# A three-layer graph attention kernel: the first layer's input split into two fp32r parts, score columns on VectorE

## What is computed

```python
def _L0_gnn_ref(h, adj, W, a):                      # layer A
    Wh = jnp.matmul(h, W)
    e_i = jnp.einsum('bnf,f->bn', Wh, a1)
    e_j = jnp.einsum('bnf,f->bn', Wh, a2)
    e = jax.nn.leaky_relu(e_i[:, :, None] + e_j[:, None, :], negative_slope=ALPHA)
    e = jnp.where(adj == 0, MASK_VAL, e)
    attention = jax.nn.softmax(e, axis=2)
    return jax.nn.elu(jnp.matmul(attention, Wh))
...
def gat_layer(x, mask, W, a_src, a_dst, bias, concat):   # layers B and C
    xl = (x @ W).reshape(B, N, H, F)
    asrc = jnp.einsum('bnhf,hf->bnh', xl, a_src)
    adst = jnp.einsum('bnhf,hf->bnh', xl, a_dst)
    e = jax.nn.leaky_relu(asrc[:, :, None, :] + adst[:, None, :, :], NEG_SLOPE)
    e = jnp.where(mask[..., None], e, NEG_INF)
    attn = jax.nn.softmax(e, axis=1)
    out = jnp.einsum('bsdh,bshf->bdhf', attn, xl)
...
x = _layernorm(x + _L0_gnn_ref(x, adj, L0_gnn_W, L0_gnn_a), axis=-1)
x = _layernorm(x + _L1_gnn_ref(adj, x, ...), axis=-1)
```

## Time and profile before

| | |
|---|---|
| median of 3 runs | 668.99 us |
| profiled execution, device time | 667.11 us |
| its span (first to last instruction) | 665.2 us |
| PE, PEld, DVE busy | 637.9, 574.9, 588.7 us (96%, 86%, 88%) |
| ACT, POOL busy | 482.0, 448.6 us (72%, 67%) |
| DMA | 45.68 MB at 69 GB/s on average |
| mean granted clock of PE | 0.988 of full speed |

### The profile page before, as it was taken

The page is one execution under the profiler, slowest core; times in us unless marked ns, Lnnn a source line. Parts: engine busy times, 40 slices in busy tenths (PEclk is TensorE's granted clock), DMA queues, the critical chain, the costliest instruction groups (busy, mean ns, idle before and its releaser), DMA issues. The chain is left out here.

```text
span 665.2 us, 17485 instructions
## 1 busy us (share of the span) xinstructions
PE 637.9 (96%) x4156; PEld 574.9 (86%) x4156; DVE 588.7 (88%) x2315; ACT 482.0 (72%) x1220; POOL 448.6 (67%) x811
## 2 busy tenths in 40 slices
PE   6979999999999999999999999999999999999993
PEld 5758899998999999999999989999999999988871
DVE  1488999999999999999999999999999999899953
ACT  1457887787778777777787777778877777687661
POOL 0247577777777777677777777777777777666762
PEclk9999999999999999999999999999999999999996
DMA  8311112222212222221122222211222222210001
GB/s 269 96 48 36 46 49 80 81 65 81 67 37 75 81 81 80 65 81 62 40 77 81 81 67 78 81 48 50 80 81 80 65 80 73 89 33 0 18 17 47
DMA packets 46693, 45.68 MB, mean 69 GB/s; under 512 B 2817, under 2 KB 46337, under 8 KB 46594
## 3 DMA queue, kind: packets, MB, share of 16 engines
q1 hardware_dynamic: 45648, 43.79, 20.8%
q10 hardware_dynamic: 946, 0.80, 0.4%
HBM read 36.19 MB, written 8.39 MB: 67 GB/s over the span
## 5 line engine op out<-in xcount | busy, mean ns | idle before, releaser
L378 POOL TENSOR_SCALAR probB<-probB,rdenB 128x256 f32<-128x256 f32 x256 | 124.7, 499 | 79.9 <-DVE rdenB L958 79.6
L558 ACT ACTIVATE probB<-probB,shiftB 128x256 f32<-128x256 f32 x256 | 127.1, 499 | 16.8 <-DVE shiftB L927 13.0
L1524 PE MATMUL PS<-probTB,VB 128*128 128x256 f32 x512 | 128.2, 382 | 0.9 <-ACT probTB L577 0.8
L941 DVE SCALAR_TENSOR_TENSOR probB<-PS,VB,gatedB 128x256 f32<-128x256 f32 x256 | 111.5, 478 | 1.8 <-issue 0.4
L389 POOL TENSOR_TENSOR inlC<-hidT,inhC 128x512 fp32r<-128x512 f32 x64 | 82.0, 1281 | 43.7 <-ACT inhC L622 43.6
L899 DVE CUSTOM_DVE_ANT_0 gatedB<-PS,gate_bc 128x256 f32<-128x256 f32 x256 | 93.8, 420 | 7.3 <-PE PS L1494 5.5
L1524 PEld LDWEIGHTS PS<-probTB,VB 128*128 128x128 f32 x512 | 89.3, 190 | 11.0 <-ACT probTB L577 2.1
L1480 PE MATMUL PS<-WhB,inhB 128*128 128x260 f32 x256 | 81.8, 319 | 1.4 <-DVE inlB L972 1.2
L577 ACT ACTIVATE probTB<-PS 128x512 f32<-128x512 f32 x128 | 72.9, 591 | 9.9 <-PE PS L1505 9.6
L360 POOL TENSOR_TENSOR y<-y,xres 128x512 f32<-128x512 f32 x32 | 41.1, 1286 | 52.4 <-DVE y L963 52.4
L1480 PE MATMUL PS<-WhC,inhC 128*128 128x258 f32 x256 | 75.4, 294 | 0.5 <-issue 0.4
(11 more groups left out here) (108 smaller groups left out, 1626.1 us busy)
## 6 DMA issues: line engine op xcount, KB each, us to landing
adj_in<-in_adj_dram SPq DMA_DIRECT2D x32, 256.0 KB, 4.3
xTin<-in_x_t_dram SPq DMA_DIRECT2D x32, 256.0 KB, 4.1
adjT_in<-in_adj_t_dram SPq DMA_DIRECT2D x32, 256.0 KB, 3.1
xres<-in_x_dram SPq DMA_DIRECT2D x32, 256.0 KB, 2.8
out_dram<-res SPq DMA_DIRECT2D x32, 256.0 KB, 2.1
WTC<-in_L_gnn_W_t_dram SPq DMA_DIRECT2D x1, 512.0 KB, 7.4
WTB<-in_L_gnn_W_t_dram ACTq DMA_DIRECT2D x1, 512.0 KB, 8.0
WB<-in_L_gnn_W_dram SPq DMA_DIRECT2D x2, 256.0 KB, 8.3
```

The lines of the kernel that those rows point to most:

```text
L378: last = pool.tensor_scalar(B.prob[h][:, k, :], B.prob[h][:, k, :], B.rden[:, k, h:h + 1], 1.0, ALU.mult, ALU.mult)
L558: last = nc.scalar.activation(L.prob[h][:, k, :], L.prob[h][:, k, :], ACT.Exp, bias=L.shift[:, k, h:h + 1], accum_out=den[:, k, h:h + 1] i ...
L941: last = nc.vector.scalar_tensor_tensor(out=L.prob[h][:, k, :], in0=PS[b][:, (h % 2) * N:(h % 2 + 1) * N], scalar=L.V[:, k, h, 1:2], in1=L ...
L1524: last = nc.tensor.matmul(PS[b][:, o:o + N], B.V[:, k, h, 2:B.F + 2], B.probT[h][:, k, :], start=(k == 0), stop=(k == NT - 1))
```

## The change

The host no longer supplies transposed weights or a packed table of vectors. The attention vectors are loaded as they are and broadcast to all partitions, and DVE makes the score columns with a multiply and a running sum. Layer A's input is split like that of B and C: `high_a` on ACT, `low_a` on POOL, and the common `project` on PE. `xTin` is free for the next load once `low_a` has run, not once both projections have. In SP's body the load of `xT` stands first. All heads stay scaled on POOL. PE issues 30 products of ones instead of 4: 18 in the fill and 12 near the end of the drain. The written-out order of all engines is another one, and with it the bank numbers.

```diff
-                        for tile in range(NT):
-                            sp.wait_ge(A.s_lin[tile][0], t.this() - 2)
+                        sp.wait_ge(s_loA, t.this() - 2)
...
+            def low_a(t):
+                if active(t):
+                    pool.wait_ge(s_hiA, t.this())
+                    if t.later:
+                        for tile in range(NT):
+                            pool.wait_ge(A.s_lin[tile][0], t.last())
+                    pool.tensor_tensor(A.inl[:, :, :], xTin[t.at % 2][:, :, :], A.inh[:, :, :].bitcast(F32), ALU.subtract)\
+                        .then_inc(s_loA, 1)
...
+            def high_a(t):
+                if active(t):
+                    act.wait_ge(s_x[t.at % 2], t.loaded())
...
+                    nc.scalar.activation(A.inh[:, :, :], xTin[t.at % 2][:, :, :], ACT.Copy).then_inc(s_hiA, 1)
...
-            def score_columns(L, b):
-                dve.wait_ge(L.s_wa, 1)
-                nc.vector.tensor_copy(L.W[:, :, :, 0:2], PS[b][:, 0:2 * L.KT * L.H]
...
+            def score_columns(L, k, heads):
...
+                        nc.vector.scalar_tensor_tensor(out=L.prod[:, j, :], in0=L.W[:, k, h, 2:L.F + 2],
+                                                       scalar=0.8 if j == 0 else -0.8, in1=v, op0=ALU.mult, op1=ALU.mult,
+                                                       accum_out=L.W[:, k, h, j:j + 1]).then_inc(L.s_wab, 1)
...
-            def score_products(L, b):
...
-                            last = nc.tensor.matmul(PS[b][:, o:o + 2], L.WT[:, h + q, k * P:(k + 1) * P], vec[:, v:v + 2],
-                                                    start=(q == 0), stop=(q == n - 1))
...
-            def project_a(tile, b, t):
...
-                    for k in range(A.KT):
-                        last = nc.tensor.matmul(PS[b][:, 0:D + 2], xTin[t.at % 2][:, k, tile * P:(tile + 1) * P], A.W[:, k, 0, :],
-                                                start=(k == 0), stop=(k == A.KT - 1))
...
-                    for s in [s_loB] if L is B else s_loC:
+                    for s in [s_loA] if L is A else [s_loB] if L is B else s_loC:
...
-                warm_up(7, 4)
-                score_products(A, 6)
...
+                warm_up(4, 2)
+                warm_up(0, 8)
+                warm_up(5, 2)
...
+                warm_up(6, 2)
+                warm_up(0, 2)
...
+                warm_up(0, 12)
```

More of the change, by code:

```diff
@@ L1157, in fill @@
[L1157 to L1171 removed]
+                inverse_sum_head(1, b2)
@@ L1237, in drain @@
-                logit(B, 2, 2, e4)
-                maxima(B, 0, 5, e4)
+                top(B, 0, e4)
+                logit(B, 1, 1, e4)
+                inverse_sum(A, 0, 5, e3)
+                make_gate_a(e2)
+                logit(B, 0, 1, e4)
+                elu_first(e3)
+                shift(B, 0, e4)
+                elu(1, 3, e5)
+                values_b(0, 1, 4, e4)
+                inverse_sum_head(0, e4)
+                values_b(1, 1, 5, e4)
+                inverse_sum(C, 0, 7, e6)
@@ L1259, in drain @@
[L1259 to L1272 removed]
+                maxima(A, 0, 2, e2)
@@ new lines, in drain @@
+                elu(0, 0, e4)
+                maxima(B, 0, 2, e3)
+                inverse_sum(A, 0, 6, e2)
+                maxima(B, 1, 2, e3)
+                inverse_sum(A, 1, 1, e2)
+                logit(B, 0, 2, e3)
+                make_gate_b(e2)
+                logit(B, 1, 2, e3)
+                top(B, 0, e3)
+                elu_first(e2)
+                shift(B, 0, e3)
+                values_b(0, 1, 3, e3)
+                elu(1, 0, e4)
+                values_b(1, 1, 2, e3)
+                inverse_sum_head(1, e3)
@@ L1350, in drain @@
-                values_b(0, 1, 1, e1)
-                elu(1, 6, e2)
+                logit(B, 0, 1, e2)
+                elu_first(e1)
+                shift(B, 0, e2)
+                elu(1, 7, e3)
+                values_b(1, 1, 0, e2)
+                values_b(0, 1, 1, e2)
+                stats(A, e1)
+                meanvar(A, e1)
+                maxima(B, 3, 7, e2)
+                inverse_sum_head(0, e2)
+                maxima(B, 2, 7, e2)
+                logit(B, 3, 7, e2)
+                top(B, 1, e2)
```

1535 lines of the change are left out of this document (754 added, 781 removed).

## The result

The changed kernel takes 671.62 us in the median (670.44 to 673.66, 7 runs), against 668.90 us (667.90 to 671.34, 7 runs) for the kernel before on the same chip: a ratio of 1.0043, 95% interval 1.0023 to 1.0064. Forecast were 659 us and a chance of 0.84 for faster. The profiled execution has a span of 669.9 us, 4.7 more than before. Only 2.7 of these are in the medians: 671.62 us is the changed kernel's median, while the profiled execution of the kernel before (667.11 us) is 1.8 under its own.

A forecast was written before the change was run, and what follows sets the result against it. PE was taken to bound the packed turns, with DVE close behind. Projection -9.0, lockstep waits +3.1, fill -2.0 and end -1.8 sum to -9.7 us, taking the predicted median 668.99 to 659.3, said as 659; range 652 to 667.

The forecast's parts named there:

- The passes: Layer A's projection on PE: twelve fp32r matmuls replace eight fp32 passes, saving 0.31 us a turn, 9.0 us over 29 batches.
- The lockstep term: In the turns, PE loses 0.10 us each to waits between DVE and PE, +3.1 us over 31 turns.
- The step I priced at nothing: In each turn, POOL's new subtraction `low_a` delays nothing, since PE wants its result half a turn later: 0 us.
- The packed stretch: Between fill and end, PE has no wait over half a microsecond: 593 us, or 31 turns.
- what PE issues sets the time there: In the packed stretch, PE's work sets the turn of 19.12 us, with DVE close behind at 18.3 us busy.
- The fill: At the start, earlier spreading, A's weighing and B's first projection save 2.0 us.
- its bound: For the fill at the start, the worst case, with DVE waiting for C's loads: +3 us.
- its sign of being wrong: In the fill, the forecast would be wrong if PE is packed only later than at 53 us.
- The end: Twelve products of ones keep PE's clock up for the last eight weighing passes, saving 1.8 us.
- the drain: Ahead of the last passes, the forecast had no term for any change: 0 us.
- POOL disturbs DVE: In the turns, `low_a` lengthens DVE's `gate_a` and `gate_bc`, +15 us, giving 680 us; chance 0.08.
- DVE keeps the turn at 19.1: In the turns, PE's 0.31 us become waits, only fill and end gain, giving 665 us; chance 0.20.

The follow-up runs named there:

- number 7: The changed kernel with A's projection in unsplit fp32, and batch 0's adjT and residual loads ahead of batch 3's xT load: 670.54 us.
- number 6: The changed kernel with DVE's shift of A moved ahead of A's weights in the steady turns: 668.09 us, ratio 0.9980 to the kernel before.
- number 5: The kernel before, its order nearly kept, with A split in 25 steady turns, B's second top and shift earlier and low_a waiting for that shift: 675.84 us.
- 8: The changed kernel with 51 more products of ones in six PE waits of the fill: 668.75 us, ratio 0.9982 to the kernel before.
- number 9: The changed kernel with B's and C's score-column products on DVE cut to 2 columns, so results are incomplete: 671.50 us.
- 1: The changed kernel without the 12 products of ones at PE's end: 674.41 us, ratio 1.0077 to the kernel before.
- 2: The kernel before with only 12 products of ones added near PE's end: 666.42 us, ratio 0.9972.
- number 13: The changed kernel with holds mended in fill, turn and drain, and ones placed anew in the fill, 14 more at the start: 661.49 us.
- 10: The changed kernel with instructions moved in fill and drain so DVE's two-input ones avoid POOL's tensor-tensors: 668.00 us.
- 11: The changed kernel with shift of A early, ones in the fill's waits, and holds removed in fill and drain: 664.32 us.

## Why the prediction was wrong, step by step

| step | forecast, us | measured, us |
|---|---|---|
| A's projection and lockstep, turns | -9.0 + 3.1 | -3.5 in 23 turns (-3.8 in 25) |
| fill | -2.0 | +6.7 up to the second marker (about 1.7 of it can be the execution's) |
| end | -1.8 | -2.0 |
| drain ahead of the last 16 us | 0 | +3.4 |
| sum | -9.7 | +4.7 (+2.7 in the medians) |

**The passes** were right in size: 12 of them take 310.07 to 311.63 = 1.56 us where 1.44 were summed, the 0.12 being at their borders. Against fp32 in the same order (number 7) the turn fell by 0.14 us and, with the hold off `shiftA`, by 0.24 (number 6).

**The lockstep term** was mis-sized: 0.10 us a turn was allowed, 0.16 was lost. Of this one held `shiftA` is 0.10 (number 6); the other 0.06 is left there too, at the borders of the passes or elsewhere. The step I priced at nothing, "`low_a`... its result is wanted by PE about half a turn later", asked only who waits for its result and not what it stops while it runs. The saving was multiplied by 29 batches and the waits by 31, besides; only 25 turns are in the steady order, and fill and drain, in which PE does not set the time, don't collect the saving. The packed stretch was also read too long: the next wait of PE over half a microsecond ends not at 643.28 but at 585.97 us, so it is 536 us or 28 turns.

```profile
585.97 0.36 PE L1480 MATMUL PS<-WhB,inhB 128*128 128x260 f32 x1 [0.64 <-DVE inlB L972]
```

And "what PE issues sets the time there" was half of it: in each turn of the old order PE's second projection of B begins 0.15 us after VectorE's `inlB` ends (number 5), so VectorE had closed the turn at the same moment, and without the new order PE's saving was worth nothing.

**The fill** is the step that failed: put at -2.0 us, it measured +6.7, and +3 was taken as its bound. Single forecasts in it came true: spread of A at 13.35 (said: before 13.5), first inverse sum at 20.76 (said: before 22.1), no wait for C's loads. The start of the first projection, 9.83 for 9.9, was partly luck: the columns could begin at 5.91, not 7.0, and a hold of 0.7 us on the weight split made up most of it. What came later did not: the x1 transposes of batch 0 at 32.70 where the kernel before has 31.1, those of the third batch at 68.0 for 65.0, and waits of PE over half a microsecond up to 95.39, far past the 53 us that the prediction gave as its sign of being wrong. The sum was made for the first 20 us, priced each instruction at its duration alone, and took PE's lost work as gain; that PE's clock falls when it has less to do stood in no term behind the first projection. What the runs showed instead (numbers 7 and 8): the split costs 4.2 us there, and about 3.1 return when the waits are filled and the clock stays up. The other 2.5 us come with the new order; holds are among them, but how much they are is open. The columns are about 1 us (number 9).

**The end** was right in mechanism and size (numbers 1 and 2), and **the drain** was not priced at all. Its 3.4 us are mostly the new order: they stay without the split (number 7), and moving three shifts there gave nothing clear (119.2 us in number 13, but 120.7 in numbers 10 and 11 with the same drain, for 120.1). What is in them stays open.

**The rivals.** "POOL disturbs DVE" had the mechanism, with a chance of 0.08 and, for the turns, the wrong victim. Its price was sought in `gate_a` (0.55 us in the median before, 0.65 after), and `elu_first`, never over 693 ns, was read as proof that two inputs in SBUF are safe. It proves nothing: in the kernel before, GpSimd waits for that very instruction, and in none of its 32 cases did anything run beside it. In number 13 one begins just behind the start of a subtraction for C and takes 1777 ns. "DVE keeps the turn at 19.1" is not what happened in the new order (18.97 us), but it is what happens in the old one (number 5): a saving on PE counted only together with an order that has room for it.

## What to carry to other kernels

An instruction that is free on its own engine may still stop another one. Before GpSimd is given work, list VectorE's instructions with two inputs in SBUF that can fall beside it, the tiny ones first, and the conversions of the gates: each waited here until GpSimd's instruction ended, whatever its own size. Moving it by one place is the cure if the one that takes its place has room behind it, as `topC` had in number 6.

A saving on the engine that leads is worth its size only in turns where that engine leads alone. An engine that is busy all the time can still be tied to another: look for the row that starts at the same place in both kernels (number 5). Price fill and drain by a marker per batch, not by their first steps.

Taking work off TensorE in a fill can slow it. Look at the granted clock of each stretch; fill the waits with ones, but count two passes per fp32 product and keep them shorter than the wait at the lower clock.
